# Graph layer and mixture of experts on one core: routed tiles as one part, weighted rows added to the output by indirect accumulating stores

## The reference

```python
# x: 12500 x 256, 212500 edges (src, dst, weight), 8 experts 256 -> 512 -> 256, top 2 of 8
h   = layernorm(x) @ gnn_W
x1  = x + segment_sum(h[dst] * edge_weight, src) + gnn_bias
xn  = layernorm(layernorm(x1)) * gamma + beta          # second one with eps inside
w   = softmax(top2(xn @ Wr + br))                       # two experts and two weights per row
out = x1 + sum over the two experts e of w_e * (gelu(xn @ W1[e] + b1[e]) @ W2[e] + b2[e])
```

## Time and profile before

| | |
|---|---|
| time, median of 3 runs | 3912.1 us (3911.53 to 3913.44) |
| the profiled execution's own time, its span | 3911.1 us |
| PE, PEld, DVE, ACT, POOL busy | 3228.5, 2117.9, 2439.0, 1362.3, 2494.5 us |
| chain that ended last | PE 43%, DVE 16%, issue 9% of the span |
| blocks, line 705 | 62 loads of 256 KB |

### The profile page before, as it was taken

One profiled execution on the slowest core, in us unless ns is written; L12 is line 12 of the kernel. 1 busy time (PEld: TensorE's weight loads), 2 busy tenths in 40 slices (PEclk: granted clock), 3 DMA queues, 4 the chain that ended last, 5 costly groups with the idle time before them and its releaser, 6 DMA issues.

```text
span 3911.1 us, 76490 instructions
## 1 busy us (share of the span) xinstructions
PE 3228.5 (83%) x21249; PEld 2117.9 (54%) x21249; DVE 2439.0 (62%) x6051; ACT 1362.3 (35%) x2894; POOL 2494.5 (64%) x2425
## 2 busy tenths in 40 slices
PE   6677776806898988989989998898988989989973
PEld 4444554503455555555555555555555556678863
DVE  9699544515566666666666667666666666445553
ACT  1353876700222222222222222222222223456642
POOL 1241588877777777777777777777777776630143
PEclk9899988957999999999999999999999999999987
DMA  4342001013434343434343434343434345452363
GB/s 153 102 126 63 26 25 30 16 33 109 118 106 124 109 120 105 122 109 121 111 118 110 118 110 120 108 117 108 116 109 120 108 116 101 141 187 86 114 182 117
DMA packets 287933, 413.94 MB, mean 106 GB/s; under 512 B 89045, under 2 KB 219930, under 8 KB 287642
## 3 DMA queue, kind: packets, MB, share of 16 engines
q0 software_dynamic: 106112, 270.68, 24.8%
q1 hardware_dynamic: 110872, 71.23, 6.4%
q10 hardware_dynamic: 70660, 68.35, 5.5%
HBM read 336.22 MB, written 73.83 MB: 105 GB/s over the span
## 4 chain that ended last, share of the span: by engine, by line
PE 43%; DVE 16%; issue 9%; DVEq 5%; POOL 3%; DMA 1%; ACT 1%; ACTq 0%; SPq 0%; POOLq 0%
PE twin L1922 9%; PE bank L1922 7%; PE twin L1852 7%; DVE area L1404 4%; PE twin L1854 3%; PE twin L1905 3%; PE bank L1905 3%; DVEq L1419 2%; POOL area L800 2%; PE twin L1990 2%; DVE area L1412 2%; PE twin L2007 2%; PE bank L1990 2%; PE bank L2007 1%; DVE rel L1401 1%
## 5 line engine op out<-in xcount | busy, mean ns | idle before, releaser
L800 POOL DMA_INDIRECT area<-h_table,listed x1856 | 1864.1, 1004 | 604.2 <-issue 543.7
L1852 PE MATMUL twin<-area 128*128 x2608 | 881.1, 386 | 74.8 <-issue 37.5
L1854 PE MATMUL twin<-area 128*128 x2608 | 718.9, 276 | 0.0
L972 ACT ACTIVATE area<-twin,b_t 128x512 f32<-128x512 f32 x208 | 142.9, 687 | 1468.6 <-PE twin L1905 821.8
L1412 DVE TENSOR_TENSOR area<-area,listed 128x1024 f16 x652 | 423.0, 690 | 107.5 <-DVE area L1404 95.2
L1852 PEld LDWEIGHTS twin<-area 128*128 x2608 | 256.9, 99 | 412.3 <-issue 183.2
L768 POOL DMA_INDIRECT edge_list<-area,didx x256 | 326.4, 1275 | 76.2 <-issue 74.7
L1922 PE MATMUL twin<-w2h,area 128*128 128x256 f16 x1664 | 355.2, 311 | 0.0
L829 POOL DMA_INDIRECT area<-ys,back_i x92 | 89.3, 971 | 334.4 <-DMA ys<-area 260.4
L1519 DVE TENSOR_TENSOR area<-area 128x512 f16<-128x512 f32 x416 | 266.7, 689 | 48.9 <-ACT area L974 48.9
L1922 PE MATMUL bank<-w2h,area 128*128 128x256 f16 x1664 | 289.5, 273 | 0.0
(11 more groups left out here) (338 smaller groups left out, 6393.1 us busy)
## 6 DMA issues: line engine op xcount, KB each, us to landing
area<-h_table,listed POOLq DMA_INDIRECT x1856
area<-in_x_dram SPq DMA_DIRECT2D x194, 128.0 KB, 2.1
area<-zs SPq DMA_DIRECT2D x62, 256.0 KB, 2.8
ys<-area ACTq DMA_DIRECT2D x62, 256.0 KB
h_table<-area SPq DMA_DIRECT2D x97, 128.0 KB, 1.7
xt<-in_x_dram ACTq DMA_DIRECT2D x97, 128.0 KB
out_dram<-area ACTq DMA_DIRECT2D x92, 128.0 KB, 2.3
area<-in_L_ffn_W_dram ACTq DMA_DIRECT2D x16, 512.0 KB, 3.9
```

Source lines behind the costliest of these rows:

```text
L800: pool.indirect_dma_start(out=stage[:, (k % RU) * UNIT + 2 * D * c:(k % RU) * UNIT + 2 * D * (c + 1)], out_offset=None, in_=h_table[:, :], ...
L1852: nc.tensor.matmul(psA[:, :], target[:, ds(at, P, 2)], stage[:, ds(rows, 2 * D)], start=False, stop=False)
L1854: last = nc.tensor.matmul(psA[:, 0:D], target[:, ds(at + TGT // 2, P, 2)], stage[:, ds(rows, D)], start=False, stop=False)
```

## The change

Routed tiles are one part, with one table of blocks: 46 + 8 = 54 blocks. Each row in `zs` gets four more words (1040 bytes instead of 1024): its row in the output, the weight of its second choice, first weight minus second, and its first expert. The weights are therefore computed in the loop (the exponentials at tile 94, the rest at tile 95). `load_z` issues a second DMA for these words. SP, not POOL, waits for the last gather, ahead of the first `load_z`; after four tiles it writes the zeros, then loads the other 42; only when all 46 are scattered are blocks loaded. DVE multiplies a block's rows by their weights as it copies them, and POOL adds them to the output with two indirect DMAs of 128 rows, one block at a time. `ys`, its stores, the gathers back, the loads of x1, the combining and the last stores go. SP's `load_block` waits for the adds of the block four before, since the output rows stand in `zin`. Cleared rows point to rows 0 to 255 after the padding and add zero to them.

```diff
+            # sp
+            reached(sp, s_gat[(RL - 1) % RU], 16 * RUN * (RL // RU) * blocks)
+            sp.sem_inc(s_gath, 1)
             def load_z(j):
                 if j >= 4:
                     sp.wait_ge(s_put[j % 4], 32 * (j // 4))
-                sp.dma_start(zt[:, j % 4, :], z_rows[j * P:(j + 1) * P, :]).then_inc(s_zt[j % 4], 16)
+                sp.dma_start(zt[:, j % 4, 0:D], z_rows[j * P:(j + 1) * P, :]).then_inc(s_zt[j % 4], 16)
+                if j == 0:
+                    sp.wait_ge(s_meta, 1)
+                sp.dma_start(zt[:, j % 4, D:PW], meta[:, j, :]).then_inc(s_zt[j % 4], 16)
             def load_block(n):
                 if n >= RZ:
                     sp.wait_ge(s_turn, n - RZ + 1)
+                    sp.wait_ge(s_share, n - RZ + 1)
+                    sp.wait_ge(s_added, 32 * (n - RZ + 1))
...
-            for j in range(R0):
-                load_z(j)
+            for j in range(4):
+                load_z(j)
             sp.wait_ge(s_agg, NT)
             # two loads of b2
-            sp.wait_ge(s_rest, 1)
-            fill_of(sp, 0)
-            for n in range(RZ):
-                load_block(n)
-            # then: three load_z of part 1, fill_of(sp, 1) behind its last, one load_block, and so on
+            fill_rows()                      # waits s_rows, s_zero; nine stores of 260 words per row
+            for j in range(4, NR):
+                load_z(j)
+            sp.wait_ge(s_fills, 16 * (NE + 1))
+            for k in range(4):
+                sp.wait_ge(s_put[k], 32 * len(range(k, NR, 4)))
+            for n in range(NBL):
+                load_block(n)
+            # pool, behind the scatters; the gathers into yg are gone
+            for n in range(NBL):
+                pool.wait_ge(s_zin[n % RZ], 16 * ring_count(n, RZ))
+                pool.wait_ge(s_yo, 2 * (n + 1))
+                if n >= 1:
+                    pool.wait_ge(s_added, 32 * n)
+                for a in range(2):
+                    pool.indirect_dma_start(
+                        out=out, out_offset=bass.IndirectOffsetOnAxis(
+                            ap=zin[:, n % RZ, a, OUT_ROW:OUT_ROW + 1].bitcast(i32), axis=0),
+                        in_=yo[:, n % 2, a, :], in_offset=None, compute_op=ALU.add).then_inc(s_added, 16)
+            # dve
+            def clear_rows():                # at step 98: zero_b, b2_z
+            def b2_rows():                   # at step 100
+                dve.wait_ge(s_b2f, 32)
...
+            def shares_of(n):                # behind block_rows(n - 1, 1)
+                dve.wait_ge(s_zin[n % RZ], 16 * ring_count(n, RZ))
+                shared(nc.vector.tensor_scalar(is_first[:, :], zin[:, n % RZ, :, FIRST_E], block_e[:, n:n + 1], None,
+                                               ALU.is_equal))
+                shared(nc.vector.tensor_tensor(is_first[:, :], is_first[:, :], zin[:, n % RZ, :, FIRST_MORE], ALU.mult))
+                nc.vector.tensor_tensor(share[:, n % 2, :], is_first[:, :], zin[:, n % RZ, :, SECOND],
+                                        ALU.add).then_inc(s_share, 1)
             def block_rows(n, a):
-                reached(dve, s_yst, 16 * (n - 1))
-                nc.vector.tensor_copy(yo[:, n % 2, a, :], psY[a][:, 0:D]).then_inc(s_yo, 1)
+                dve.wait_ge(s_share, n + 1)
+                reached(dve, s_added, 32 * (n - 1))
+                nc.vector.tensor_scalar(yo[:, n % 2, a, :], psY[a][:, 0:D], share[:, n % 2, a:a + 1], None,
+                                        ALU.mult).then_inc(s_yo, 1)
```

More of the change, by code:

```diff
@@ L110, in gnn_moe_layer_kernel @@
     NR = len(routed)
-    R0 = 2 * NR // 3
-    parts = [R0, NR - R0]
     BLK = 2 * P
     RZ = 4
[L115 to L118, removed]
+    NBL = NR + NE
+    CPE = -(-NR * P // BLK) + 1
     EROWS = CPE * BLK
-    PROWS = NE * EROWS + BLK
-    LAST = [routed[R0 - 1], routed[NR - 1]]
+    ZROWS = NE * EROWS + BLK
+    LAST = routed[NR - 1]
+    PW = D + 4
+    OUT_ROW, SECOND, FIRST_MORE, FIRST_E = D, D + 1, D + 2, D + 3
+    NQ = -(-NR // SB)
+    assert all(routed[j] == 2 * SB * (j // SB) + SB + j % SB for j in range(NR)) and begins[0] == 0
     ctx = ExitStack()
@@ L198, in gnn_moe_layer_kernel @@
         upto = sb("upto", [P, NE], fp32)
[L199 to L206, removed]
+        block_no = sb("block_no", [P, NBL], fp32)
+        behind = sb("behind", [P, NBL, NE], fp32)
+        behind_n = sb("behind_n", [P, NBL, NE], fp32)
+        block_e = sb("block_e", [P, NBL], fp32)
+        block_s = sb("block_s", [P, NBL], fp32)
+        row_i = sb("row_i", [P, NBL], i32)
+        expert_i = sb("expert_i", [P, NBL], i32)
+        fill_i = sb("fill_i", [P, NE], i32)
+        is_first = sb("is_first", [P, 2], fp32)
+        share = sb("share", [P, 2, 2], fp32)
         before_h = sb("before_h", [P, P], fp16)
@@ L263, in gnn_moe_layer_kernel @@
         accr = node(fp32, 2, D)
-        zt = node(fp32, 4, D)
+        zt = node(fp32, 4, PW)
         blk = Carve()
-        zin = blk(fp32, RZ, 2, D)
+        zin = blk(fp32, RZ, 2, PW)
         zT32 = blk(fp32, KD, BLK)
@@ L491, in gnn_moe_layer_kernel @@
         s_route = sem("s_route")
-        s_backs = sem("s_backs")
+        s_zero = sem("s_zero")
+        s_meta = sem("s_meta")
+        s_rows_i = sem("s_rows_i")
+        s_share = sem("s_share")
+        s_shared = sem("s_shared")
         s_rest = sem("s_rest")
@@ L516, in gnn_moe_layer_kernel @@
         s_yo = sem("s_yo")
[L517 to L522, removed]
+        s_added = sem("s_added")
         def reached(eng, s, value, gate=True):
@@ L589, in quad_b2, with routed_before @@
             return c * (NE + 1)
[L591 to L599, removed]
+        def routed_before(t, p):
+            return len([r for r in routed if r < t and r % 2 == p])
         block = ctx.enter_context(nc.Block())
@@ L982, in exps, with routed_exps @@
                 nc.scalar.activation(unused[:, :], ones_f[:, 0:1], ACT.Gelu).then_inc(s_table, 1)
+            def routed_exps():
+                act.wait_ge(s_diffr, NR)
+                nc.scalar.activation(ex_r[:, :], diff_r[:, :], ACT.Exp).then_inc(s_expr, 1)
+                nc.scalar.activation(unused_r[:, :], ones_f[:, 0:1], ACT.Gelu)
             def weights_T(c):
@@ L1022, in _ @@
                         exps(set_of[t][0])
+                    if t == LAST + 1:
+                        routed_exps()
             store_set(NSET - 1)
[L1024 to L1027, removed]
             def turned(n):
@@ L1119, in _ @@
             nc.vector.tensor_copy(unit_no[:, :], iota_i[:, 0:NU])
-            nc.vector.tensor_copy(block_no[:, :], iota_i[:, 0:NBP])
-            for h in range(2):
-                nc.vector.tensor_scalar(ebase[:, h, :], iota_i[:, 0:NE], float(EROWS), float(h * PROWS), ALU.mult, ALU.add)
+            nc.vector.tensor_copy(block_no[:, :], iota_i[:, 0:NBL])
+            nc.vector.tensor_scalar(ebase[:, :], iota_i[:, 0:NE], float(EROWS), None, ALU.mult)
             nc.vector.tensor_scalar(tile_no[:, :], iota_i[:, 0:NT], float(P), float(P), ALU.mult, ALU.add)
@@ L1610, in step @@
             def step(t):
                 i = t - SB
+                if t == NT:
+                    clear_rows()
+                if t == NT + 2:
+                    b2_rows()
                 if t < NT:
@@ L1621, in step @@
                     slots(t - 1)
-                    if t - 1 in LAST:
-                        blocks_table(LAST.index(t - 1))
-                        back_rows(LAST.index(t - 1))
+                    if t - 1 == LAST:
+                        blocks_table()
                 if 0 <= i < NEX:
@@ L1708, in _ @@
                     block_rows(n - 1, 1)
-                for j in combined_by(n):
-                    combine(j)
+                shares_of(n)
             for a in range(2):
                 block_rows(NBL - 1, a)
-            for j in range(combined_before(NBL), NR):
-                combine(j)
         @block.tensor
@@ L1885, in ranks @@
                 pe.wait_ge(s_both, 2 * j + 2)
-                first = j in (0, R0)
+                first = j == 0
                 ins = nc.tensor.matmul(psR, before_h[:, :], both[:, :], start=True, stop=first)
```

200 lines of the change are left out of this document (70 added, 130 removed).

## The result

| | before | after |
|---|---|---|
| time, median of 4 runs each | 3912.8 us (3911.5 to 3915.6) | 3878.4 us (3876.4 to 3883.4) |
| the profiled execution's span | 3911.1 us | 3878.1 us |
| first turn (the blocks begin) | 3432.76 | 3454.40 |
| from one block to the next | 6.16, while combining 8.61 | 7.41 |
| blocks | 62 | 54 |

The ratio is 0.9913, 95% interval 0.9899 to 0.9926: 34 us faster. The forecast said 3842 us, 71 us faster. The sign was right and the time lies in the range, nearest to rival 2; but only half of the forecast gain came: 34 of 71 us.

What follows compares the result with a forecast made beforehand. PE was taken to bound the dense stage and undisturbed blocks, afterwards the adds' round trip through `zin`. 3911.1 + 25.7 (start) - 52.5 (blocks) - 43.3 (tail) = 3841.0, median 1.0 above: 3842 us; range 3802 to 3901.

Steps and rivals of the forecast that it cites:

- rival 2: In the block loop and tail, the adds take 5 to 6.5 us to land; 3891 us, chance 0.16.
- Start: Before the blocks, all 46 tiles are scattered first; first turn at 3458.5 instead of 3432.76, +25.7 us.
- Dense stage: Before the blocks, `b2_rows` delays PE's end by 8 to 12 us, to near 3424, at no cost.
- Blocks: Block loop: 53 intervals of 6.81 us, 360.9 instead of 413.4 us, -52.5 us.
- its wake-up: In the block loop, POOL starts the first add 0.1 us after a block's last copy.
- the issuing of an add: In the block loop, POOL issues an accumulating DMA in the same 1.3 us as today's scatters.
- the disputed landing: In the block loop and tail, an add into the output takes 4.0 us to land.
- POOL's own wait: In the block loop, POOL waits until the adds of the block before have landed; asks only 5.4 us per block.
- the bounds of L: Limits on an add's landing time in the block loop: 2.7 us below, 7.3 us above.
- PE bounds them: Undisturbed blocks of the kernel before run at PE's own pace, 6.16 us each, PE busy 258.6 of 264.6 us.
- rival 1: In the block loop, adds land within 3.2 us and PE keeps its pace; 3806 us, chance 0.24.
- Tail: Behind the last product: copy, wake-up, issue, landing and closing take 9.0 instead of 52.3 us, -43.3 us.

Runs made afterwards that it cites:

- e8: Kernel before with all 46 routed tiles in one part, 54 blocks, still stored, gathered back and combined; 3924.6 us, ratio 1.0033.
- e11: e8 with ACT's store of a block issued one block later; 3908.7 us, ratio 0.9990 against the kernel before.
- e10: Changed kernel with `b2_rows` moved behind the step loop; 3880.3 us, ratio 0.9915 against the kernel before.
- e4: Changed kernel, four buffers, output rows copied out of `zin` by DVE, block load not waiting for adds; 3844.4 us, ratio 0.9824 against the kernel before.
- e7: Changed kernel with five input buffers and plain indirect stores in place of the adds; 3804.7 us, ratio 0.9724 against the kernel before.
- e1: Changed kernel with plain indirect stores in place of the adds, sum left out; 3835.2 us, ratio 0.9804 against the kernel before.
- e3: Changed kernel with a ring of three input blocks instead of four; 4325.0 us, ratio 1.1057 against the kernel before.
- e2: Changed kernel with a ring of five input blocks instead of four; 3842.8 us, ratio 0.9826 against the kernel before.

## Why the prediction was half right

It summed to 3841.0 for the profiled execution; 3878.1 came, 37.1 more. By its own steps:

**Start: 25.7 forecast, 21.6 measured (-4.1).** The steps behave as told: first scatter behind SP's wait, a hole behind the eighth (6.68 us, not 3: the eighth scatter ends at 3334.97, SP asks for the next tile at 3335.63, and its scatter starts 6.0 later), about 2.6 us per tile, one wake-up and one load. That the sum came out low is chance: the last gather starts 6.57 us earlier. Counted from it the first turn comes 142.6 us behind, where the forecast says 140.2. In the variants of the changed kernel the last gather starts 3.9 to 9.2 us earlier than in the one trace of the kernel before. It also does in e8 (2.9) and e11 (6.4), which have one part but none of the change's other edits, and which differ from each other only in the blocks. So some 3 us of this is how executions differ; what the rest is, is open.

**Dense stage: forecast end near 3424, measured 3418.8.** The stall behind `b2_rows` is there (8.05 us at line 1898) and is hidden, as told; e10, in which PE has no such wait, confirms that it is free.

**Blocks: pace 6.81 forecast, 7.41 measured (53 x 0.60 = +32.0).** This is the step that failed, by the size of its terms (with the tail, below, whose wait and closing were also too small). The mechanism is the one forecast: rings of 3, 4 and 5 and e4 all move as the loop says. Two terms of POOL's were too small, its wake-up (0.1 forecast, 0.75 measured) and the issuing of an add (1.3 forecast, 1.86 measured), and the disputed landing was right. The round trip was 13.62 in the forecast. Taken from the starts and ends in the trace after, for the adds of the blocks 1 to 49 (the first is block 0), in us:

| | forecast | median | mean |
|---|---|---|---|
| turn to the end of the last copy | 4.58 | 4.30 | 4.45 |
| to the first add | 0.1 | 0.75 | 0.92 |
| to the second add | 1.3 | 1.86 | 1.86 |
| to the turn that it frees: landing, SP, load, PE | 7.64 | 7.45 | 7.75 |

The means add to 14.98, 7.49 per block (7.41 over all 53, for the first and last blocks are quicker). Against 6.81 that is + 0.41 per block for the way from copy to add, + 0.28 for the issue, + 0.05 for landing and load, - 0.06 for the turn. The 0.41 are the wake-up (0.33) and, in 17 blocks, POOL's own wait for the adds before. The turn is quicker by median, which fits that ACT's stores no longer stand ahead of its gelus (shown by e11 for the kernel with one part, not here), and late in the five blocks where PE's matmuls run at its lower clock behind a wait (6.87 at most; mean clock 0.97). The forecast put SP's way from event to issue at 0.74, from a row, and POOL's at 0.1, from none. The forecast took the issuing of an add "at the same 1.3", and left a doubling to the bounds of L.

**The floor: "PE bounds them" was wrong.** PE was busy for 98% of the undisturbed stretch, and that was read as PE's pace. e7 and e11 run at 5.89 and 5.90. It changed nothing in this forecast, whose pace lay above 6.16, but rival 1 was priced 53 x 0.27 = 14 us too high by it: with landings of 2.5 and five buffers, e7 is at 5.89.

**POOL's own wait: "asks only T > 1.4 + L = 5.4".** With the same two terms mis-sized it asks 0.77 + 1.90 + 3.85 = 6.52. With four buffers it decides only in those 17 blocks; with five it is the bound (6.57).

**Tail: 9.0 forecast, 17.9 measured (+8.9).** The last add was taken to follow the last copy at once. But the last copies of the last two blocks are 3.28 us apart, as DVE's last rows show, where the adds of one block start 6.3 behind those of the block before (3859.14 and 3865.44 above):

```profile
3856.91 0.48 DVE L1657 TENSOR_SCALAR area<-bank,share 128x256 f32<-128x256 f32 x1
...
3860.19 0.48 DVE L1657 TENSOR_SCALAR area<-bank,share 128x256 f32<-128x256 f32 x1 [0.93 <-PE bank L1965]
```

So the last block's adds wait for those of the block before, and the last one starts at 3867.30, 7.15 behind the last product, where 1.9 was forecast: 1.2 of this is wake-up and issue, 4.0 the wait. It lands at 3871.05, and the end is 7.0 us behind that, where 3.1 was forecast. These 7.0 are POOL's `DRAIN` of 6.60 us and 0.4 around it. The 3.1 had been worked out from ACT's last store, but the end of the kernel before was set by POOL's `DRAIN` too, 8.1 us behind the end of its last gather (8.1 in e8 and e11 as well). In the changed kernel POOL first waits for its adds to land, and only then drains. From the last landing to the end it is 7.0 with the ring of 3, 4 or 5 and 9.6 with plain stores (e1 and e7), so the adding does not make it; what the `DRAIN` waits for, and whether it ends sooner without the wait ahead of it, was not tried.

**From the last cast to the last product:** 10.66 against 10.51. The four add up: -4.1 + 32.0 + 0.1 + 8.9 = 36.9 of the 37.1.

Two bounds of the forecast do not follow from its own terms: L = 5 gives 3869.5, not 3866, and L = 6.2 gives 3902.5, not 3901. Neither touches the comparison.

## What to carry to other kernels

When a buffer is freed only by a DMA that writes somewhere, the pace is the whole round trip divided by the buffers between: write out every term, and give each wake-up and each issue a row or a bound, not only the landing that looks risky. First ask whether the freed thing can be let go earlier (here two words per row, copied out, gave the same as a fifth buffer). An engine that is 98% busy may still be waiting a little in each round: look at what each round waits for before calling it the bound. And look at what really ended last in the program, not at the last transfer that you know of.

## What the runs showed of the hardware

- An indirect add into DRAM of 128 rows of 1 KB costs 1.554 us of POOL and lands in 3.8 us (108 adds of after); the same DMA as a plain store costs 0.970 and lands in 2.5 (e1). The prediction's estimate of 2.6 for an add, made from the Trainium skill's "DMA: Bandwidth & Descriptors" ("Anatomy of one DMA — SWDGE (gpsimd) path") and "Collectives: The Full Stack" ("The bandwidth ceiling: the fold count and why AG ≠ RS ≠ AR"), is 1.2 us too low: the trace disagrees. For the plain store the 2.0 us plus bytes over 436 KB per us of the same section of the Trainium skill's "DMA: Bandwidth & Descriptors" gives an estimated 2.3, near the 2.5 of e1.
- POOL starts an indirect DMA 0.75 to 0.78 us after the event that it waited for in most rounds of after, be it a landing or a DVE instruction, where the next on a running POOL starts 0.30 after the end of the last.
- PE's granted clock is lower where PE rests more: beside 15.85 us per block it is 0.71 in the mean (e3), beside 7.41 it is 0.97 (after), and with PE full it is 1.00 (e7).
- Behind its last indirect DMA POOL's closing `DRAIN` goes on: 6.60 us after the landing of the last add (after, e2), 9.22 after that of the last plain store (e1, e7), and until 8.1 us behind the last gather where POOL had not waited for its landing (before, e8, e11).
